# Constants on TensorE between stages, and rows scattered a step sooner, in a four-layer kernel with routed experts

## The chip, the cores and the metric

The kernel runs on one core of one Trainium2 chip. The metric is the time of one execution on the device in microseconds (us); lower is better. The engines are PE (TensorE), DVE (VectorE), ACT (ScalarE), POOL (GpSimd) and SP (SyncE, which here only issues transfers); "PEq" and "SPq" are their sequencers.

## The reference, cut to what matters

The input x is 128 sequences of 64 tokens with 128 features. Four layers follow one another. Each is a cross attention against a second input, added to x with a gate, and a feed-forward part, added with a gate:

```
x = x + tanh_gate * attention_l(layernorm(x), ctx)     # four kinds: wide heads, 16 heads of 8, masked, "stablemax"
x = x + tanh_gate * feed_forward_l(layernorm(x))
# l0: 8 experts, 128 -> 512 -> 128, one expert a token, GELU, capacity
# l1: one dense quantised network
# l2: 8 experts, two experts a token, gated SiLU, weights of the two from a softmax
# l3: 8 experts, one expert a token, ReLU, capacity, scaled by the gate's probability
```

A token's expert comes from a product of its normalised row with a small router matrix; its place ("slot") in the expert's list comes from a running count over all tokens before it.

## The kernel before, in words

The 8192 tokens are 64 tiles of 128. x stays in SBUF. There are seven long stages, one after another, each a block with a program for each engine: `attention_wide` (named l0 below), `experts` (experts0), `attention_split` three times (l1, l2, l3; l1 also carries the dense network, the `follower`), and between them `experts` again (experts2 between l2 and l3, experts3 after l3). A block ends when all engines have arrived: no engine starts the next stage before that, except for transfers of weights that were asked for early.

`attention_wide` works in 64 items of one tile, `attention_split` in 32 items of two tiles. An engine's program is a software pipeline: in step t it does part s for item t - s. In `attention_split` the parts are STAT 1, NORM 2, TURN 3, PROJ 4, SCORE 5, then PROB 6, OUT 7, STREAM 8 in l3 ("stable") and PROB 7, OUT 8, STREAM 9 in l2 ("folded") and l1. The waits between engines are on semaphores, and each engine runs its own list strictly in order.

`Router` is the tail of l0, l2 and l3. For part s of it DVE takes statistics of the finished rows (`bn_stats`, L702; `bn_aggr`, L754), POOL adds epsilon (L624) and takes the root (L629), DVE normalises (L759, written into the rows that will be sent), PE turns and scores them, and once for each batch of items DVE chooses the expert (L726 to L749), PE counts (L642 to L646), and a step later DVE turns the counts into slots (L712 to L719, the tile `put`). POOL then sends the rows to the slots in DRAM with indirect transfers (L617, one for each tile and expert of the token). A batch is 8 tiles, 4 items, in l3, and 4 tiles, 2 items, in l2. In l3 POOL's step is: eps and root for the attention's own norm (L916, L921), the same for the router (L624, L629), `combine` of the rows that came back from experts2 (L397, L401, L403), a wait for PE's output of the step (`o_filled`, L1277), then L617. In l2 L617 stands at the head of the step. In l3 DVE's step is: L1026, L674/L670, L991, L978/L982 (statistics of the item that `combine` has just finished), L1039/L1041, L966, the router's part (L702, slots, choice, L754, L759), L1061.

In l2 `Weigh` follows the last slots on DVE (L452 to L511): it turns the routing into a table of tiles and weights.

`experts` multiplies tiles of sent rows by weights: transposes (L1976), the first product (L1968; four matmuls of f32, 128 rows by 512 columns, or twice as many by 256 in experts2), the activation, and the second (L1986; matmuls of f32, 128 by 128). A matmul of f32 is two records in the trace, a transpose one.

Of the kernel before, what the change touches and what calls it, by code (L numbers as in the profile page):

```python
# [6 lines left out]
P = 128  # L7
ALU = mybir.AluOpType
# [106 lines left out]
def pipeline(eng, items, depth, emit, unroll=2):  # L115

    for t in range(items + depth - 1):
        emit(Step(eng, items, t))


def wait(eng, sem, count):
# [407 lines left out]
class Router:  # L529
# [57 lines left out]

    def depth(self):

        return 5 + self.nb  # L590

    def totals(self, nc, dve):

# [5 lines left out]
    def scatter(self, nc, pool, t, s):  # L599

        g, k = self.g, self.tiles
        out = s + 4 + self.nb
        sent_before = t.landed(out + 2, k * self.ks)

        slotted = t.batches(out - self.nb + 1 + (t.t - out) % self.nb, self.nb) if t.live(out) else None
        if t.live(out):

            if self.slots_clear and t.t == out:

                pool.wait_ge(*self.slots_clear)  # L610
            for tile in range(t.item(out) * k, t.item(out) * k + k):
                for c in range(self.ks):

                    if c == 0 and tile % k == 0:
                        wait(pool, self.put_done, slotted)
                        wait(pool, self.sent[t.par(out)], sent_before)
                    pool.indirect_dma_start(  # L617
                        self.slots, bass.IndirectOffsetOnAxis(ap=g.put[c][:, tile:tile + 1], axis=0), g.row[:, tile, self.sent_cols], None,
                        bounds_check=self.slots.shape[0] - 1, oob_is_err=False).then_inc(self.sent[t.par(out)], 16)
# [56 lines left out]
    def dve(self, nc, dve, t, s, updated, n_updated, read, n_read):  # L676
# [21 lines left out]
        if t.live(s):  # L698

            wait(dve, updated, n_updated)  # L700
            for tile in range(k):
                last = V.bn_stats(self.st[:, t.par(s), tile, :], g.x[:, bass.ds(t.item(s) * k + tile, 1), :])  # L702
            last.then_inc(self.part, 1)
        if batch4:

            link = self.chain(slotted, "slots")
            wait(dve, read, n_read)
            if self.kind == "top2":
                then(V.tensor_tensor(self.ranked[:, :, :], self.counts[:, :, :], over(self.base[:, :]), ALU.add), *link())
            for c in range(self.ks):  # L710
                src = self.ranked if self.kind == "top2" else self.counts
                then(V.tensor_tensor(self.cand[:, :, :], self.hot[c][:, :, :], src[:, :, :], ALU.mult), *link())  # L712
                then(V.tensor_reduce(self.rank[:, :], self.cand[:, :, :], AX.X, ALU.add), *link())
                if self.kind != "top2":

                    V.tensor_scalar(self.lost[:, :], self.rank[:, :], float(CAP), NOWHERE, ALU.is_gt, ALU.mult)
                    then(V.tensor_tensor(self.slot[:, :], self.rank[:, :], self.expert_base[:, :], ALU.add), *link())
                    then(V.tensor_tensor(self.rank[:, :], self.slot[:, :], self.lost[:, :], ALU.add), *link())
                last = V.tensor_copy(g.put[c][:, tiles(s + 4)], self.rank[:, :])  # L719
            last.then_inc(self.put_done, 1)  # L720
        if batch3:
# [26 lines left out]
                V.tensor_scalar(self.expert_base[:, :], self.best[:, :], -float(CAP), float(EXPERTS * CAP - 1), ALU.mult, ALU.add)  # L748
                last = V.tensor_copy(self.chosen[:, :, :], self.hot[0][:, :, :])  # L749
            last.then_inc(self.chosen_done, 1)  # L750
        if t.live(s):
            wait(dve, self.part, n0)
            for tile in range(k):
                last = V.bn_aggr(self.mv[:, t.par(s), tile, :], self.st[:, t.par(s), tile, :])  # L754
            last.then_inc(self.stats, 1)
        if t.live(s + 1):
            wait(dve, self.rstd_done, n1)
            for tile in range(k):
                last = V.tensor_scalar(  # L759
                    g.xn[:, t.item(s + 1) * k + tile, :], g.x[:, t.item(s + 1) * k + tile, :],  # L760
                    self.mv[:, t.par(s + 1), tile, 0:1], self.rstd[:, t.par(s + 1), tile:tile + 1], ALU.subtract, ALU.mult)
            last.then_inc(self.xn_done, 1)

    def chain(self, count, name):

# [13 lines left out]
def attention_split(nc, g, name, gate_col, kind, head=None, stream=None, router=None, together=None, weights=None, out=None, follow=None):  # L779
# [13 lines left out]
    with ExitStack() as ctx:  # L793
# [112 lines left out]
        @block.gpsimd  # L906
        def _(pool):
            def step(t):
                if folded:

                    wait(pool, scored, t.done(SCORE))
                    tail.scatter(nc, pool, t, T0)
                if t.live(NORM):

                    wait(pool, stats_done, t.done(NORM))
                    nc.gpsimd.tensor_tensor(var_eps[:, t.par(NORM), :], mv[:, t.par(NORM), :, 1], g.eps[:, 0:2], ALU.add).then_inc(eps_done, 1)  # L916
                if tail:
                    tail.add_eps(nc, pool, t, T0 + 1)
                if t.live(NORM):
                    wait(pool, eps_done, t.done(NORM))  # L920
                    nc.gpsimd.tensor_tensor(rstd[:, t.par(NORM), :], var_eps[:, t.par(NORM), :], g.neg_half[:, 0:2],  # L921
                                            ALU.pow).then_inc(rstd_done, 1)
                if tail:
                    tail.root(nc, pool, t, T0 + 1)
                if head and t.live(1):
                    head.combine(nc, pool, t, 1)

                if stable:

                    wait(pool, o_filled, t.done(OUT))  # L930
                    tail.scatter(nc, pool, t, T0)

            for t in range(max(ITEMS + (T0 + tail.depth() if tail else NORM + 1) - 1, FOLLOW + follower.STEPS if follower else 0)):
                if t == 10:
                    ph.clear_old()
                if follower is None or t < STEPS:
                    step(Step(pool, ITEMS, t))
                if following(t):
                    follower.gpsimd(pool, t - FOLLOW)
                    if t == FOLLOW + 16:  # L940

                        pool.wait_ge(follower.y_added, 1)
                        ph.clear_first(own)
            if tail:
                tail.finish(pool, ITEMS)

        @block.vector
        def _(dve):
# [119 lines left out]
                    tail.dve(nc, dve, t, T0, wo_drained, t.done(T0), ranks_drained, beats(t.t, T0 + 3, RANKS_BEATS))  # L1068

            for t in range(FOLLOW + follower.STEPS if follower else STEPS):  # L1070
                if t == 3:
                    prepare()
                    dve.wait_ge(ready, 1)
                if t < STEPS:
# [79 lines left out]
        def _(pe):  # L1154
# [188 lines left out]
            def handed_over(u):  # L1343
# [6 lines left out]
                if u == follower.HT_FIRST:  # L1350
                    pe.wait_ge(wo_drained, ITEMS)
                    pe.wait_ge(turned_drained, TURNED_BEATS)

            for t in range(FOLLOW + follower.STEPS if follower else STEPS):
                if t == 4:
                    pe.wait_ge(ready, 1)
                if t < STEPS:
                    step(Step(pe, ITEMS, t))
                if following(t):
                    handed_over(t - FOLLOW)  # L1360
                    follower.tensor(pe, t - FOLLOW)
            if weigh:
                weigh.tensor(nc, pe)


def attention_wide(nc, g, t_in, router, dropped, later):
# [7 lines left out]
    with ExitStack() as ctx:  # L1374
# [88 lines left out]
        def _(pool):  # L1463
            def step(t):
# [6 lines left out]
                if t.live(0):  # L1471
# [4 lines left out]
                    wait(pool, eps_done, n0)  # L1476
                    nc.gpsimd.tensor_tensor(rstd[:, t.par(0):t.par(0) + 1], var_eps[:, t.par(0):t.par(0) + 1],
                                            g.neg_half[:, 0:1], ALU.pow).then_inc(rstd_done, 1)
                tail.scatter(nc, pool, t, 8)
                tail.add_eps(nc, pool, t, 8)  # L1480
                tail.root(nc, pool, t, 8)

            ph.clear_old()
            pipeline(pool, ITEMS, 8 + tail.depth(), step, UNROLL)
# [111 lines left out]
        def _(pe):  # L1596
# [98 lines left out]
                    last.then_inc(misc_filled, 1)  # L1695

            pipeline(pe, ITEMS, DEPTH + 5, step, UNROLL)

def experts(nc, g, name, slots, rows, w1, b1, w2, b2, kind, gate_col, last=False, early=None):
# [2 lines left out]

    dynamic, gated = kind == "silu", kind == "relu"
    HALVES = 2 if dynamic else 1
    ITEMS = TOP2_TILES // 2 if dynamic else SLOT_TILES  # L1710
    WIDTH, SUBS = SLOTS // HALVES, SUB // HALVES
# [4 lines left out]
    with ExitStack() as ctx:  # L1716
# [53 lines left out]

        @block.sync
        def _(sp):
            def step(t):
                n3, n4 = t.done(3), t.done(4)

# [5 lines left out]

                if t.live(0):

                    wait(sp, xt_filled, n4)
                    wait(sp, idx_ready, n4)
                    if not dynamic:
                        wait(sp, based, n4)
                    for h in range(HALVES):
                        sp.dma_start(xs[:, t.par(0, XS), h * SUBS:h * SUBS + SUBS, :], rows_of(0, h).rearrange("(s p) d -> p s d", p=P)).then_inc(  # L1789
                            x_in[t.par(0, XS)], 16)  # L1790
                if t.live(1):

                    wait(sp, h_filled[3], t.done(1 + WS))
                    if not dynamic:
                        wait(sp, h_drained[3], n3)
                    for h in range(HALVES):
                        sp.dma_start(w1_s[:, t.par(1, WS), h, :, :], at(w1_v, expert(sp, t, 1, h))).then_inc(w1_in[t.par(1, WS)], 16)  # L1797
                    if not dynamic:
                        sp.dma_start(b1_s[:, t.par(1), :], b1[bass.ds(expert(sp, t, 1, 0), 1)].rearrange("a f c -> (a f) c")).then_inc(
                            w1_in[t.par(1, WS)], 16)  # L1800
                if t.live(2) and not dynamic:
                    load_w2(sp, t, 2)
                    sp.dma_start(b2_s[:, t.par(2), :], b2[bass.ds(expert(sp, t, 2, 0), 1)].partition_broadcast(P)).then_inc(
# [147 lines left out]
        def _(pe):  # L1951
# [38 lines left out]
            def both(t):  # L1990
                step(t)
                if early:
                    early.tensor(pe, t.t)

            pe.wait_ge(go, 1)
            pipeline(pe, ITEMS, DEPTH, both)

# [331 lines left out]
```

## Time and profile before

| | us |
|---|---|
| median of 3 runs (lowest to highest) | 2513.36 (2510.45 to 2514.68) |
| the profiled execution's own time | 2513.01 |
| its span, first to last instruction | 2511.2 |

| stage | from, us | to, us | PE busy | granted clock |
|---|---|---|---|---|
| l0 | 5.7 | 779.4 | 716.05 | 0.98 |
| experts0 | 779.4 | 919.5 | 124.56 | 0.95 |
| l1 | 919.5 | 1379.5 | 355.66 | 0.84 |
| l2 | 1379.5 | 1791.1 | 346.18 | 0.88 |
| experts2 | 1791.1 | 2020.9 | 208.76 | 0.95 |
| l3 | 2020.9 | 2366.6 | 272.94 | 0.87 |
| experts3 | 2366.6 | 2511.2 | 122.61 | 0.92 |

The granted clock is that of TensorE, as a share of 2.4 GHz; 0.50 is 1.2 GHz. The mean over the span is 0.915. A stage's time is set by whatever chain of work ends last in it, so an engine's busy share alone does not say what bounds it.

### The profile page before, as it was taken

To read this page: it belongs to the slowest core of one execution; us is meant where nothing else is said; L and a number is where in the kernel's file an instruction comes from. 1 tells how busy PE (TensorE), PEld (TensorE's weight loads), DVE (VectorE), ACT (ScalarE), POOL (GpSimd) and SP (SyncE) were. 2 spreads that over 40 slices of the span, in tenths; PEclk is the share of its full clock that TensorE was granted. 3 is DMA by queue.
4 is the path that set the end of the run, shared out by engine and by line. 5 is a ranking of instruction groups with operands and counts; after the bars stand their busy time and mean duration, and the time that the engine had idled before them with its cause. 6 is when DMAs were issued, how large, how long until landed. Compare 5 with 4: busy or idle time off the path is not lost. (4 is left out here: it accounts for less than half of the span.)

```text
span 2511.2 us, 81208 instructions
## 1 busy us (share of the span) xinstructions
PE 2146.8 (85%) x33432; PEld 1717.8 (68%) x33443; DVE 1787.9 (71%) x5105; ACT 1350.6 (54%) x2499; POOL 1157.7 (46%) x1712
## 2 busy tenths in 40 slices
PE   6999999999995969999555799998399958898597
PEld 5887878787874746777444577776399947777375
DVE  3777777777773648887896589886555559988354
ACT  3555555555551327886998455553122259979232
POOL 1333333434343541113776125555466666876444
PEclk8999999999997979998677899997699979989699
DMA  6330000000005621110000111111487622332363
GB/s 194 110 123 27 25 27 25 24 21 20 20 18 152 180 85 55 55 58 17 1 1 3 32 37 52 52 51 36 134 235 230 185 75 79 106 96 79 101 185 103
DMA packets 225233, 195.14 MB, mean 78 GB/s; under 512 B 34444, under 2 KB 197846, under 8 KB 224864
## 3 DMA queue, kind: packets, MB, share of 16 engines
q1 hardware_dynamic: 186336, 143.52, 19.6%
q0 software_dynamic: 18944, 36.98, 4.2%
q10 hardware_dynamic: 19584, 9.44, 1.3%
q8 instruction: 265, 4.34, 0.8%
q14 instruction: 104, 0.85, 0.1%
HBM read 113.53 MB, written 70.55 MB: 73 GB/s over the span
## 5 line engine op out<-in xcount | busy, mean ns | idle before, releaser
L617 POOL DMA_INDIRECT slots<-row,put x256 | 258.1, 1008 | 211.5 <-issue 131.2
L1968 PE MATMUL experts_H<-experts_xs_t,experts_w 128*128 128x256 f32 (+1 forms) x832 | 253.5, 456 | 9.9 <-DMA experts_w<-in_F_w 4.7
L1102 ACT ACTIVATE l_prob_t<-l_banks 128x512 f32<-128x512 f32 x256 | 132.2, 603 | 145.9 <-PE l_banks L1219 115.4
L1968 PEld LDWEIGHTS experts_H<-experts_xs_t,experts_w 128*128 128x128 f32 x832 | 156.7, 195 | 74.5 <-issue 54.0
L1474 POOL TENSOR_TENSOR l_var_eps<-l_mv,eps 128x1 f32<-128x1 f32 x64 | 12.1, 189 | 413.9 <-DVE l_mv L1555 413.9
L1277 PE MATMUL l_banks<-l_val,l_prob_t 128*64 128x18 f32 x5120 | 201.1, 215 | 0.0
L1277 PEld LDWEIGHTS l_banks<-l_val,l_prob_t 128*64 128x64 f32 x5120 | 190.3, 143 | 8.1 <-issue 0.7
L1510 DVE TENSOR_REDUCE l_top<-l_S 128x16 f32<-128x1024 f32 x64 | 78.3, 1224 | 161.7 <-PE l_S L1653 161.7
L1986 PE MATMUL experts_Y<-experts_w,experts_hid 128*128 128x128 f32 x1600 | 190.0, 275 | 3.5 <-DVE experts_y L1912 2.6
L1986 PEld LDWEIGHTS experts_Y<-experts_w,experts_hid 128*128 128x128 f32 x1600 | 184.3, 192 | 5.0 <-issue 4.9
L1823 POOL DMA_INDIRECT rows<-experts_y,experts_idx x144 | 139.9, 971 | 90.0 <-DVE experts_y L1908 52.9
L1012 DVE TENSOR_REDUCE l_top<-l_banks 128x32 f32<-128x2048 f32 x64 | 146.5, 2288 | 46.3 <-PE l_banks L1226 33.7
L916 POOL TENSOR_TENSOR l_var_eps<-l_mv,eps 128x2 f32<-128x2 f32 x96 | 24.3, 253 | 302.3 <-DVE l_mv L982 218.7
L1944 ACT ACTIVATE experts_hid<-experts_H,experts_b_scaled 128x512 f32<-128x512 f32 x128 | 80.0, 687 | 135.2 <-DVE experts_b_scaled L1864 115.7
L1619 PE MATMUL l_R<-l_ctx_t,l_wk 128*128 128x128 f32 x1024 | 134.2, 286 | 11.6 <-DMA l_ctx_t<-in_ctx_t 11.6
L1619 PEld LDWEIGHTS l_R<-l_ctx_t,l_wk 128*128 128x128 f32 x1024 | 122.5, 196 | 19.9 <-issue 18.3
L1469 POOL TENSOR_TENSOR l_prob<-l_prob,l_recip 128x1024 f32<-128x1024 f32 x64 | 121.3, 1895 | 24.6 <-DVE l_recip L1506 24.6
L1941 ACT ACTIVATE experts_act_gate<-experts_H 128x512 f32<-128x512 f32 x72 | 43.0, 597 | 163.3 <-PE experts_H L1968 163.3
L1567 ACT ACTIVATE l_q_t<-l_R 128x512 f32<-128x512 f32 x128 | 76.4, 597 | 96.9 <-PE l_R L1619 96.9
L1619 PE MATMUL l_R<-l_xn_t,l_wq 128*128 128x128 f32 x1024 | 126.5, 277 | 2.0 <-DVE l_xn_t L1527 2.0
L1690 PE MATMUL l_R<-l_wo,l_out_t 128*64 128x128 f32 x2048 | 126.1, 276 | 0.0
L1111 ACT ACTIVATE l_k_m<-l_banks,early_bk_masked,const_table 128x256 f32<-128x256 f32 x256 | 124.9, 595 | 0.0
(312 smaller groups left out, 5943.4 us busy)
## 6 DMA issues: line engine op xcount, KB each, us to landing
experts_w<-in_F_w SPq DMA_DIRECT2D x136, 256.0 KB
l_ctx_t<-in_ctx_t SPq DMA_DIRECT2D x96, 128.0 KB, 2.4
early_q_m<-l_q_t SPq DMA_DIRECT2D x384, 32.0 KB, 1.8
experts_xs<-slots SPq DMA_DIRECT2D x72, 132.0 KB
experts_w<-in_F_w ACTq DMA_DIRECT2D x72, 128.0 KB, 3.3
slots<-l_empty SPq DMA_DIRECT2D x16, 536.0 KB, 4.1
experts_xs<-slots SPq DMA_DIRECT2D x16, 536.0 KB
slots<-l_empty SPq DMA_DIRECT2D x16, 520.0 KB, 5.9
```

Source lines behind the costliest of these rows:

```text
L617: pool.indirect_dma_start(self.slots, bass.IndirectOffsetOnAxis(ap=g.put[c][:, tile:tile + 1], axis=0), g.row[:, tile, self.sent_cols], No ...
L1012: V.tensor_reduce(top[:, :, :].rearrange("p r a -> p (r a)"), X[:, :, :].rearrange("p r (a k) -> p (r a) k", k=64), AX.X, ALU.max).then_in ...
L1102: nc.scalar.activation(prob_t[:, t.par(PROB), r, :], Z[:, r, :], ACT.Exp).then_inc(prob_done, 1)
L1111: last = nc.scalar.activation(k_m[:, t.par(PROJ, SLOTS_QK), j, :], QK[:, 256:512], ACT.Identity, bias=bk_masked[:, j:j + 1], scale=g.const ...
L1277: last = nc.tensor.matmul(O[64 * tile:64 * tile + 64, 18 * h:18 * h + 18], term[:, t.par(OUT), h // 4, col:col + 64], val[:, t.par(OUT), t ...
L1469: nc.gpsimd.tensor_tensor(prob[:, t.par(5, 4), :, :, :], prob[:, t.par(5, 4), :, :, :], recip[:, t.par(5), :, :].unsqueeze(3).broadcast_to ...
L1619: last = nc.tensor.matmul(R[:, BANK[name], P * k:P * k + P], w[:, 4 * (c % 2) + k, :], moving, start=True, stop=True)
L1690: last = nc.tensor.matmul(MISC[64 * b:64 * b + 64, P:2 * P], out_t[:, t.par(7), k, b, :], wo_s[:, b, k, :], start=k == 0, stop=k == 7)
L1823: pool.indirect_dma_start(rows, bass.IndirectOffsetOnAxis(ap=idx[:, t.par(4, XS), k:k + 1], axis=0), y[:, t.par(4), k, :], None, bounds_ch ...
L1944: nc.scalar.activation(hid[:, t.par(2), c, :], H[:, c, :], ACT.Gelu if kind == "gelu" else ACT.Relu, bias=b1_scaled[:, t.par(2), c:c + 1], ...
L1968: last = nc.tensor.matmul(H[:, c, cols], w1_s[:, t.par(2, WS), h, c, :], xs_t[:, t.par(2), cols], start=True, stop=True)
L1986: last = nc.tensor.matmul(Y[:, P * k:P * k + P], hid[:, t.par(3), c, P * k:P * k + P], w2_s[:, t.par(3, WS), k // SUBS, c, :], start=c == ...
```

## The change

`keep_active` is a new function: a given number of matmuls of a constant by itself, into a bank that nothing reads. PE calls it before the loop of `attention_split` (16 times, in l3 40), after its steps 3 to PROB - 1 (10 each), in l2 and l3 after each of the last steps (8 each) and at the end (70 in l2, 50 in l3), at the end of l0 (34), before the first item of each `experts` stage (14), after step 1 of experts2 (12), and at the end of experts0 (45) and experts2 (55).

The router's rows are sent a step sooner: the depth is 4 + nb where it was 5 + nb (nb is the number of items in a batch), so the first item of a batch is sent in the same step in which DVE writes its slots. In l2 and l0 L617 moves to the end of POOL's step. DVE's part of the router now has L759 and L754 ahead of slots and choice. `prepare()`, DVE's clears, is called at t == 0 and not at t == 3. In experts2 SP asks for an item's first weights ahead of its rows, a step sooner.

```diff
+def keep_active(nc, g, out, count):
+    ident = g.const[:, C_IDENT:C_IDENT + P]
+    for _ in range(count):
+        nc.tensor.matmul(out, ident, ident, start=True, stop=True)
...
     def depth(self):
-        return 5 + self.nb
+        return 4 + self.nb
...
-        out = s + 4 + self.nb
+        out = s + 3 + self.nb
...
             last.then_inc(self.part, 1)
+        if t.live(s + 1):
+            wait(dve, self.rstd_done, n1)
...
+            last.then_inc(self.xn_done, 1)
+        if t.live(s):
+            wait(dve, self.part, n0)
...
+            last.then_inc(self.stats, 1)
         if batch4:
...
         if batch3:
...
-        if t.live(s):
-            wait(dve, self.part, n0)
...
-        if t.live(s + 1):
-            wait(dve, self.rstd_done, n1)
...
             def step(t):
-                if folded:
-                    wait(pool, scored, t.done(SCORE))
-                    tail.scatter(nc, pool, t, T0)
...
+                if folded:
+                    wait(pool, scored, t.done(SCORE))
                     tail.scatter(nc, pool, t, T0)
...
-                if t == 3:
+                if t == 0:
                     prepare()
...
+            IDLE = Z[:, 3, 0:P]
+            keep_active(nc, g, IDLE, 40 if head else 16)
...
+                if TURN <= t < PROB:
+                    keep_active(nc, g, IDLE, 10)
+                if t >= ITEMS + OUT - 1 and not follower:
+                    if t == ITEMS + OUT - 1:
+                        pe.wait_ge(plus_done if stable else prob_done, 4 * ITEMS)
+                    keep_active(nc, g, IDLE, 8)
...
             if weigh:
                 weigh.tensor(nc, pe)
+            if not follower:
+                keep_active(nc, g, IDLE, 70 if weigh else 50)
...
-                tail.scatter(nc, pool, t, 8)
                 tail.add_eps(nc, pool, t, 8)
                 tail.root(nc, pool, t, 8)
+                tail.scatter(nc, pool, t, 8)
...
             pipeline(pe, ITEMS, DEPTH + 5, step, UNROLL)
+            pe.wait_ge(drained["k1"], ITEMS)
+            keep_active(nc, g, R[:, 1, 0:P], 34)
...
+            def load_w1(t, s):
+                wait(sp, h_filled[3], t.done(s + WS))
+                for h in range(HALVES):
+                    sp.dma_start(w1_s[:, t.par(s, WS), h, :, :], at(w1_v, expert(sp, t, s, h))).then_inc(w1_in[t.par(s, WS)], 16)
...
                 if t.live(0):
+                    if dynamic:
+                        load_w1(t, 0)
...
+                if dynamic and t.t == 1:
+                    keep_active(nc, g, Y[:, 0:P], 12)
+            keep_active(nc, g, Y[:, 0:P], 14)
             pe.wait_ge(go, 1)
             pipeline(pe, ITEMS, DEPTH, both)
+            if not end:
+                pe.wait_ge(xt_drained, ITEMS)
+                keep_active(nc, g, X[:, 0:P], 55 if dynamic else 45)
```

## Rows read from the trace of the kernel before

**Rows 1.** Page, granted TensorE clock in 40 slices of the span, in tenths.

```profile
PEclk8999999999997979998677899997699979989699
```

**Rows 2.** Stretches, stages l2 and l3: us, busy of engines, clock, DMA share, GB/s.

```profile
1379.50:1791.10 411.60, 346.18 (x6353) 260.71 (x6353) 324.99 (x1142) 190.93 (x452) 182.50 (x256) 0.88 0.15 46
...
2020.90:2366.60 345.70, 272.94 (x4904) 224.55 (x4904) 273.58 (x809) 261.81 (x417) 237.35 (x320) 0.87 0.28 85
```

**Rows 3.** Timeline of POOL, l3, step with L719 and the next: start, us.

```profile
2158.64 0.73 POOL L403 TENSOR_TENSOR row<-row,l_term 128x256 f32<-128x256 f32 x1
...
2159.54 1.06 POOL L617 DMA_INDIRECT slots<-row,put  x1 [0.17 <-issue]
...
2163.07 0.20 POOL L624 TENSOR_TENSOR l_tail_var_eps<-l_tail_mv,eps 128x2 f32<-128x2 f32 x1 [0.96 <-DVE l_tail_mv L754]
...
2165.84 1.17 POOL L397 TENSOR_TENSOR l_term<-l_got,weight 128x256 f32<-128x256 f32 x2
...
2168.01 0.72 POOL L403 TENSOR_TENSOR row<-row,l_term 128x256 f32<-128x256 f32 x1
```

**Rows 4.** Timeline of DVE in the same stretch.

```profile
2159.40 0.49 DVE L978 BATCH_NORM_STATS2 l_st<-row 128x6 f32<-128x128 f32 x2
...
2162.67 0.17 DVE L719 CAST put<-l_rank 128x8 uint32<-128x8 f32 x1
...
2162.91 0.57 DVE L759 TENSOR_SCALAR row<-row,l_tail_mv,l_tail_rstd 128x128 f32<-128x128 f32 x2
```

**Rows 5.** Timeline, l0 to experts0.

```profile
770.12 0.19 PE L646 MATMUL l_R<-l_before,const_bf 128*128 128x32 bf16 x1
...
779.50 0.15 DVE L1838 TENSOR_SCALAR experts_gate_c<-gates 128x1 f32<-128x1 f32 x1 [7.85 <-PEq L1374]
...
785.66 5.85 PE L1968 MATMUL experts_H<-experts_xs_t,experts_w 128*128 128x512 f32 x8 [1.29 <-DMA experts_b<-in_F_b]
...
796.71 3.51 PE L1986 MATMUL experts_Y<-experts_w,experts_hid 128*128 128x128 f32 x30
```

**Rows 6.** Timeline of DVE and POOL, end of l2.

```profile
1755.89 0.60 DVE L759 TENSOR_SCALAR row<-row,l_tail_mv,l_tail_rstd 128x128 f32<-128x128 f32 x2 [1.69 <-POOL l_tail_rstd L629]
...
1770.57 0.17 DVE L719 CAST put<-l_rank 128x4 uint32<-128x4 f32 x1
...
1787.46 0.25 DVE L511 TENSOR_SCALAR weight<-l_weigh_second,gates 128x64 f32<-128x64 f32 x1
...
1788.48 0.97 POOL L617 DMA_INDIRECT slots<-row,put  x1 [0.30 <-issue]
```

**Rows 7.** Timeline, experts2's first and last matmuls.

```profile
1801.28 6.62 PE L1968 MATMUL experts_H<-experts_xs_t,experts_w 128*128 128x256 f32 x16 [4.67 <-DMA experts_w<-in_F_w]
...
1809.35 3.72 PE L1968 MATMUL experts_H<-experts_xs_t,experts_w 128*128 128x256 f32 x16 [1.01 <-DVE experts_xs_t L1878]
...
2008.83 2.02 PE L1986 MATMUL experts_Y<-experts_w,experts_hid 128*128 128x128 f32 x16 [0.88 <-DVE experts_y L1908]
```

**Rows 8.** Timeline, experts0's last matmuls; L1012 in l1.

```profile
909.73 1.50 PE L1986 MATMUL experts_Y<-experts_w,experts_hid 128*128 128x128 f32 x12
...
949.06 2.29 DVE L1012 TENSOR_REDUCE l_top<-l_banks 128x32 f32<-128x2048 f32 x1 [2.14 <-PE l_banks L1210]
...
958.12 2.29 DVE L1012 TENSOR_REDUCE l_top<-l_banks 128x32 f32<-128x2048 f32 x1 [3.15 <-PE l_banks L1210]
...
965.24 2.29 DVE L1012 TENSOR_REDUCE l_top<-l_banks 128x32 f32<-128x2048 f32 x1 [0.39 <-PE l_banks L1210]
```

**Rows 9.** Timeline of DVE, start of l2, the clears of prepare().

```profile
1382.12 0.54 DVE L953 MEMSET l_val<- 64x576 f32 x1
...
1384.04 0.49 DVE L978 BATCH_NORM_STATS2 l_st<-row 128x6 f32<-128x128 f32 x2
```

**Rows 10.** Timeline of l3: last L1277 of a step, the L617 after it.

```profile
2140.50 0.30 PE L1277 MATMUL l_banks<-l_val,l_prob_t 128*64 128x18 f32 x4
...
2141.59 1.06 POOL L617 DMA_INDIRECT slots<-row,put  x1 [0.77 <-PE l_banks L1277]
```

More of the change, by code:

```diff
@@ L703, in dve @@
             last.then_inc(self.part, 1)
+        if t.live(s + 1):
+            wait(dve, self.rstd_done, n1)
+            for tile in range(k):
+                last = V.tensor_scalar(
+                    g.xn[:, t.item(s + 1) * k + tile, :], g.x[:, t.item(s + 1) * k + tile, :],
+                    self.mv[:, t.par(s + 1), tile, 0:1], self.rstd[:, t.par(s + 1), tile:tile + 1], ALU.subtract, ALU.mult)
+            last.then_inc(self.xn_done, 1)
+        if t.live(s):
+            wait(dve, self.part, n0)
+            for tile in range(k):
+                last = V.bn_aggr(self.mv[:, t.par(s), tile, :], self.st[:, t.par(s), tile, :])
+            last.then_inc(self.stats, 1)
         if batch4:
@@ L750, in dve @@
             last.then_inc(self.chosen_done, 1)
-        if t.live(s):
-            wait(dve, self.part, n0)
-            for tile in range(k):
-                last = V.bn_aggr(self.mv[:, t.par(s), tile, :], self.st[:, t.par(s), tile, :])
-            last.then_inc(self.stats, 1)
-        if t.live(s + 1):
-            wait(dve, self.rstd_done, n1)
[L758 to L762, printed above, removed]
     def chain(self, count, name):
@@ L930, in step @@
                     wait(pool, o_filled, t.done(OUT))
+                    tail.scatter(nc, pool, t, T0)
+                if folded:
+                    wait(pool, scored, t.done(SCORE))
                     tail.scatter(nc, pool, t, T0)
@@ L1697, in _ @@
             pipeline(pe, ITEMS, DEPTH + 5, step, UNROLL)
+            pe.wait_ge(drained["k1"], ITEMS)
+            keep_active(nc, g, R[:, 1, 0:P], 34)
 def experts(nc, g, name, slots, rows, w1, b1, w2, b2, kind, gate_col, last=False, early=None):
-    dynamic, gated = kind == "silu", kind == "relu"
+    dynamic, gated, end = kind == "silu", kind == "relu", last
     HALVES = 2 if dynamic else 1
@@ L1790, in step @@
                             x_in[t.par(0, XS)], 16)
[L1791 to L1800, printed above, removed]
+                if t.live(1) and not dynamic:
+                    wait(sp, h_drained[3], n3)
+                    load_w1(t, 1)
+                    sp.dma_start(b1_s[:, t.par(1), :], b1[bass.ds(expert(sp, t, 1, 0), 1)].rearrange("a f c -> (a f) c")).then_inc(
+                        w1_in[t.par(1, WS)], 16)
                 if t.live(2) and not dynamic:
```

## The prediction

> **What bounds the kernel now.** I read the page first. Its clock line [rows 1] is at 9 tenths or full almost everywhere and falls to 6 to 8 tenths in slices near the changes of stage; the mean is 0.915, as if 427 of the 2511 us had run at half speed (0.085 / 0.5 of them). So there is something to regain, but only where TensorE at half speed is what ends last. Then I cut the span at the stages. The reader is to see in [rows 2] that PE is busy for 346 of 412 us in l2, but for only 273 of 346 in l3, where DVE (274), ACT (262) and POOL (237) are nearly as full as PE: l3 is a ring of four engines, in which none is idle long enough to swallow a late neighbour. Then I took the timeline of single engines, at one full step of l3 [rows 3, 4] and at the ends and beginnings of stages. In l3 POOL's `combine` of a step ends (L403), DVE's statistics start at once (L978), the work goes over PE and ACT and comes back to POOL as "o_filled". POOL's step is L617 twice (scatter), L916/L624/L921/L629 (eps and roots), then L397 to L403. From one L403 to the next it is 9.37 us [rows 3].
>
> The change of stage is a barrier. POOL is its last comer nearly everywhere: in l0 PE's last matmul ends at 770.31 and DVE is let go at 779.50 after 7.85 us of waiting [rows 5]; in l2 the last L617 ends at 1789.45, the last DVE instruction at 1787.71 [rows 6], and the stage ends at 1791.1 [rows 2].
>
> **The price of a constant matmul.** One is f32, 128 by 128, like those of L1986: 30 records, two for each matmul, took 3.51 us [rows 5], so 0.234 us at full clock. At half clock the double, 0.47; the same ratio shows between 6.62 and 3.72 us for the same 16 records of L1968 [rows 7].
>
> **Part 1, constants at the ends and starts of stages.** Each group has two effects: PE may reach the barrier later, and the first work of the next stage may run at full clock.
> - l0 to experts0. 34 from 770.31 would end at 778.3 if all were warm, at 786.3 if none was. They begin cold. I take 780.2 against a stage end of 779.4, +0.8 (bounds 0 and +6.9). The first L1968 took 5.85 us [rows 5] and is the same amount of columns as 3.72 [rows 7]: -2.1. Net -1.3.
> - experts0 to l1. PE's last matmul ends at 911.23 [rows 8]; 45 warm ones end at 921.8, 2.3 past the stage's end of 919.5. In l1's fill the steps of L1012 are 9.06 us and then 7.12 [rows 8]; two such steps at 1.9 less give -3.9. Net -1.6 (bounds -4 and +2.3).
> - l1 to l2. The same -3.8 at the fill. Against it stand the clears: here x is in SBUF already, so DVE's first statistics wait for the 1.92 us from 1382.12 to 1384.04 [rows 9], +1.9; and after steps 3 to 6 ten constants each, 2.3 us, which PE's waits for DVE mostly cover; I take one that is half uncovered, +1.1. Net -0.8 (bounds -4 and +3). In l1 and l3 the clears lie beside the first transfers and cost nothing; uncovered they would be another 1.9 each.
> - experts2's start. The weights are now asked for ahead of the rows. L1968 starts 4.67 us late because of experts_w [rows 7]; the weights come earlier by as much as the rows come later on the same queue, and the 12 constants stand in what is left, so I leave the start where it is, and only the clock gains: 6.62 to 3.72, -2.9 (bounds -6 and 0).
> - experts2 to l3. PE ends at 2010.85 [rows 7]; 55 constants end at 2023.7, 2.8 past 2020.9 [rows 2]. The first steps of l3 are paced by POOL's combines, so the warm clock gives back less than in l1: -2.2. Net +0.6 (bounds -3 and +3).
> - l3 to experts3: as after l0, the first L1968 at full clock, -2.1 (bounds -2.3 and 0).
>
> The rows say that after an idle stretch PE runs at 1.2 GHz and later at 2.4: the same 16 records took 6.62 and then 3.72 us [rows 7]. The Trainium skill ("TensorE: Matmul & The Clock Gate", Part 1: The HAM clock gate) says the array is throttled by default and that activity releases it; the pair agrees. It adds that the ramp penalty is under 1% of a typical span. By that last rule alone these groups could give back at most 25 us; by my rows they give back 17.
>
> **Part 2, rows sent a step sooner.** This is the part that costs. The item that is scattered is now the first of the batch whose slots DVE writes (L719) in the same step. In l3 that makes POOL, right after L403, wait for L719. Before, the scatter of that step started at 2159.54, 0.17 us after POOL's work before it [rows 3]. DVE's L978 can start only when L403 has ended (2159.40), and L719 ended at 2162.84; DVE's L759 and L754, which followed it until 2163.48 [rows 4], now stand before it, so L719 ends at 2163.48. From such a release to L617's start it is 0.79 us (2140.80 to 2141.59 [rows 10]). L617 so starts at 2164.27, 4.7 late. Behind it on POOL stand the second L617, both roots, and the combine of the next step, for which DVE waits. Given back are the 0.96 us for which L624 waited for L754 [rows 3], now done early; that leaves 3.8. The step after can save part of the 0.77 of [rows 10] (about 0.6, as 0.17 is what is left when nothing is late), and the choice step before it saves some 0.4, since the aggregate comes ahead of the choice. I take +2.8 a batch. The 32 items make eight batches, and the slots of five are written while items still come in (steps 15, 19, 23, 27 and 31): +14 (bounds: +0.8 each if the ring has slack that I don't see, +3.8 each if none; 4 and 19).
>
> In l2 POOL's sequence of instructions is the same as before, since the scatter only moves from the head of a step to the tail of the one before, and DVE waits there less than it works; nothing in the steady part. At its end, however, DVE's L759 already waits 1.69 us for POOL's root [rows 6], and POOL's root stands behind four L617. With L759 ahead of the slots, the slots are written after that wait, POOL then waits for the slots, and its next root is late: the two engines alternate instead of overlapping. Over the last three batches I estimate some 3 us for the first wait and as much again for the last batch's slots (L719 at 1770.57), from which the weighing follows (until 1787.71 [rows 6], 17.1 us of DVE). POOL's last L617 had 1.7 us more. I take +5 for the stage (bounds 0 and +9). The 70 constants behind it are 16.4 us of PE beside those 17.1 of DVE and are hidden. In l3's end the same alternation meets one batch less and a POOL that is already saturated with scatters, +2 (bounds 0 and +6); its 50 constants (11.7 us) run beside them. In l0 the batch is small and POOL is idle half the time: 0.
>
> **Sum.** -1.3 -1.6 -0.8 +5 -2.9 +0.6 +14 +2 -2.1 = +12.9. The profiled execution took 2513.0 us (its span is 2511.2), the median of the runs is 2513.4, so the two agree. 2513.0 + 12.9 = 2526.
>
> **Rivals.**
> A, faster: the new wait on L719 is hidden. The part of the ring that is ahead of POOL would need 3.8 us of slack at each batch. For it: POOL's busy share of l3 is only 237 of 346 us [rows 2]. Against it: DVE starts L978 within 0.1 us of L403's end. Then 14, 5 and 2 fall away, and the rest stays: -8.1, 2505. The deciding point is whether L617 in those steps can start within 1 us of L403. The Trainium skill (same page, HAM oscillation) speaks for this side: each idle stretch between bursts of matmuls throttles the array and the ramp is paid again, so filling them should pay; the trace agrees with the throttling and no row here prices it beyond the terms above.
> B, no change: the waits cost half of what I take (about 1.4 a batch and +2 at l2's end): +12.9 -7 -3 = +2.9, 2516. For it: the step ahead of each such step is the one in which DVE also makes the choice, and a late POOL may be caught up there.
> C, slower still: the constants don't hold the clock up. The 34 of l0 then cost the whole +6.9 (6.1 more), and if only a third of the 17.1 us of clock gains is lost, that is 6 more: 2538. The point from which it decides is the duration of the first L1968 after a group, 5.85 or 3.7. Against it: nothing is denser than matmuls back to back, and 1809.35 ran at 3.72 after 8 us of looser work [rows 7].
>
> **Chances and range.** The forecast (waits cost 8 us or more) 0.50, A 0.25, B 0.15, C 0.10. A measurement here tells 0.2%, 5 us, from no change: faster 0.25, same 0.15, slower 0.60. The range reaches from a little under A to C, 2502 to 2538; the forecast's own is 2519 to 2534.
>
> **What would show it.** Right: in l3, at each L719, L617 idle for about 4 us and released by DVE's put, and the next L978 waiting some 3 us longer for L403; L759 ahead of L719; l2 about 5 us longer from its last L1277 to the weighing's end; first L1968 near 3.7 in all three expert stages. Wrong: l3 no longer than 346 us, or a half-clock stretch still over the expert stages' starts, or PE's sequencer named as the last comer at barriers with more than 3 us.

## The result, and the profile after

| | before | changed |
|---|---|---|
| median, us | 2511.9 (2508.7 to 2514.7, 4 runs) | 2545.4 (2540.4 to 2555.4, 4 runs) |
| ratio | | 1.015, 95% interval 1.0124 to 1.0175 |
| profiled execution: span, granted clock | 2511.2, 0.915 | 2546.3, 0.942 |

The change makes the kernel about 33 us slower. The direction was forecast; the size (+13) was not, and 2545 lies outside the range of 2502 to 2538. TensorE's mean clock rose all the same. The stages of the two profiled executions, cut at the first instruction after each barrier:

| stage | before, us | changed, us | difference | sum of my terms |
|---|---|---|---|---|
| l0 | 779.5 | 779.6 | +0.1 | +0.8 |
| experts0 | 140.2 | 140.1 | -0.1 | +0.2 |
| l1 | 459.9 | 454.9 | -5.0 | -3.9 |
| l2 | 411.7 | 423.6 | +11.9 | +4.2 |
| experts2 | 229.6 | 231.1 | +1.5 | -0.1 |
| l3 | 345.8 | 372.9 | +27.1 | +13.8 |
| experts3 | 144.5 | 144.0 | -0.5 | -2.1 |

The stretches of the two stages that grew most answer to [rows 2] (us; busy of PE, PEld, DVE, ACT and POOL; clock, DMA share, GB/s):

```profile
1374.62:1798.25 423.63, 388.80 (x6717) 307.26 (x6718) 324.56 (x1142) 191.29 (x452) 181.95 (x256) 0.92 0.15 45
...
2029.40:2402.27 372.87, 321.63 (x5257) 273.22 (x5257) 264.85 (x810) 262.30 (x417) 225.47 (x320) 0.89 0.26 79
```

PE's busy time grew by 49 us in l3. The constants are 33 of them (no_constants, below, has 288.25); DVE's, ACT's and POOL's busy time fell or stayed. So the 27 us are not more work on those three. The timeline of POOL in the changed kernel at the step that answers to [rows 3] (new line numbers: L624 is the scatter that was L617, L410 is the combine's L403):

```profile
2169.68 0.73 POOL L410 TENSOR_TENSOR row<-row,l_term 128x256 f32<-128x256 f32 x1
2176.58 1.23 POOL L624 DMA_INDIRECT slots<-row,put  x1 [6.17 <-issue]
...
2182.81 0.72 POOL L410 TENSOR_TENSOR row<-row,l_term 128x256 f32<-128x256 f32 x1
```

And DVE's there (L985 was L978, L738 was L719), which answers to [rows 4]:

```profile
2171.36 0.47 DVE L985 BATCH_NORM_STATS2 l_st<-row 128x6 f32<-128x128 f32 x2
...
2175.57 0.17 DVE L738 CAST put<-l_rank 128x8 uint32<-128x8 f32 x1
...
2183.57 0.49 DVE L985 BATCH_NORM_STATS2 l_st<-row 128x6 f32<-128x128 f32 x2 [2.80 <-POOL row L410]
```

POOL idles 6.17 us for the slots, which are written at 2175.74; the scatter starts 0.84 later. From one L410 to the next it is 13.13 us where it was 9.37 [rows 3]. The wait has "issue" as its releaser: what ends it is a semaphore wait of the queue that the profile doesn't resolve, and only DVE's timeline shows which. The wait is longer than forecast (4.7 late, so 4.9 of idle) for a reason that the same rows show. The forecast let DVE's statistics start at once after the combine; here L410 ends at 2170.41 and L985 starts 0.95 later, because DVE is still at earlier parts of its own list. From L985's start to the slots it is then 4.38, where the forecast had 4.08.

Two steps later PE itself is late: POOL's scatter in that step waits for it. That row, then the stretch's clock:

```profile
2198.31 1.06 POOL L624 DMA_INDIRECT slots<-row,put  x1 [6.42 <-PE l_banks L1284]
```

```profile
2184.13:2201.19 17.06, 16.01 (x187) 12.91 (x187) 10.36 (x33) 8.80 (x15) 9.45 (x13) 0.50 0.23 71
```

The granted clock falls to 0.50, 1.2 GHz, 7.6 us after the late scatter began, and stays there for 17 us, of which PE is busy for 16.0. Before the fall PE had been busy for 10.9 of the 13.1 us of the stalled step, and in the whole of the next step it is for 6.0 of 8.3. The step after that took 14.26 us where it was 8.60. The kernel before has such a stretch too, without any wait for slots, around a step of 13.32 us:

```profile
2233.90:2250.90 17.00, 16.24 (x187) 12.90 (x187) 11.88 (x37) 8.89 (x16) 9.72 (x14) 0.50 0.33 100
```

At l3's end, timelines of DVE, POOL and PE in the changed kernel (L714 was L759, L668 scores the router's rows, L125 is the constant):

```profile
2378.76 0.60 DVE L714 TENSOR_SCALAR row<-row,l_tail_mv,l_tail_rstd 128x128 f32<-128x128 f32 x2 [4.14 <-POOL l_tail_rstd L636]
```

```profile
2375.39 1.04 POOL L624 DMA_INDIRECT slots<-row,put  x1 [5.89 <-issue]
...
2389.32 0.97 POOL L624 DMA_INDIRECT slots<-row,put  x1 [2.89 <-issue]
```

```profile
2379.97 3.62 PE L125 MATMUL l_banks<-const_table 128*128 128x128 f32 x16
2383.38 0.86 PE L668 MATMUL l_banks<-l_router_w,l_tail_xn_t 128*128 128x8 f32 x4
...
2386.87 14.98 PE L125 MATMUL l_banks<-const_table 128*128 128x128 f32 x132
2402.27 3.36 PE L125 MATMUL experts_Y<-const_table 128*128 128x128 f32 x28 [0.41 <-PEq L800]
```

POOL waits for slots (5.89), DVE for POOL's root (4.14), eight constants at half clock (3.62) stand ahead of the scores that DVE needs for the next choice, and POOL waits again (2.89). Then 66 constants in a row end 0.4 us before everybody is let go: PE is the last comer at this barrier, POOL's last scatter having ended 3.0 before it (1.8 was usual).

Two of three starts became warm. The first products of experts0 and experts2 are to be set beside [rows 5] (5.85) and [rows 7] (6.62); that of experts3, the last row, took 5.76 before and is still mostly at half clock:

```profile
785.74 3.67 PE L1990 MATMUL experts_H<-experts_xs_t,experts_w 128*128 128x512 f32 x8 [1.85 <-DMA experts_b<-in_F_b]
...
1810.18 3.62 PE L1990 MATMUL experts_H<-experts_xs_t,experts_w 128*128 128x256 f32 x16
...
2408.44 5.37 PE L1990 MATMUL experts_H<-experts_xs_t,experts_w 128*128 128x512 f32 x8 [1.80 <-DMA experts_b<-in_F_b]
```

### The profile page after: what moved, and what is told of

It reads as the page before. It is cut to its first block and busy times, and to the rows that moved or that the text cites. A ratio compares the mean times of both kernels' runs of the same rounds, so it can differ in the third digit from the quotient of the medians.

```text
span 2546.3 us, 83624 instructions
## 1 busy us (share of the span) xinstructions
PE 2279.6 (90%) x34647; PEld 1859.2 (73%) x34647; DVE 1777.0 (70%) x5105; ACT 1351.6 (53%) x2499; POOL 1146.7 (45%) x1712
## 5 line engine op out<-in xcount | busy, mean ns | idle before, releaser
L624 POOL DMA_INDIRECT slots<-row,put x256 | 259.1, 1012 | 272.1 <-issue 210.2
L1990 PE MATMUL experts_H<-experts_xs_t,experts_w 128*128 128x256 f32 (+1 forms) x832 | 247.9, 448 | 6.4 <-DMA experts_b<-in_F_b 3.7
L1845 POOL DMA_INDIRECT rows<-experts_y,experts_idx x144 | 140.2, 973 | 90.2 <-DVE experts_y L1930 53.5
L1636 PE MATMUL l_R<-l_ctx_t,l_wk 128*128 128x128 f32 x1024 | 134.1, 285 | 10.4 <-DMA l_ctx_t<-in_ctx_t 10.4
L1636 PEld LDWEIGHTS l_R<-l_ctx_t,l_wk 128*128 128x128 f32 x1024 | 122.5, 196 | 18.7 <-issue 17.1
```

The costliest lines, as they stand in the source:

```text
L624: pool.indirect_dma_start(self.slots, bass.IndirectOffsetOnAxis(ap=g.put[c][:, tile:tile + 1], axis=0), g.row[:, tile, self.sent_cols], No ...
L1636: last = nc.tensor.matmul(R[:, BANK[name], P * k:P * k + P], w[:, 4 * (c % 2) + k, :], moving, start=True, stop=True)
L1845: pool.indirect_dma_start(rows, bass.IndirectOffsetOnAxis(ap=idx[:, t.par(4, XS), k:k + 1], axis=0), y[:, t.par(4), k, :], None, bounds_ch ...
L1990: last = nc.tensor.matmul(H[:, c, cols], w1_s[:, t.par(2, WS), h, c, :], xs_t[:, t.par(2), cols], start=True, stop=True)
```

## The experiments

Eleven kernels were run. Ratios are to the kernel before on the same chip. The stages come from each kernel's one profiled execution, cut like the table above. "Last combine" is the start of the last L410 (L403) after the start of l3; "rest" is what follows until the stage's end; all columns from l2 on are in us. A profiled execution can lie up to 11 us from its kernel's median: those of late_scatter and best took 2499.3 and 2487.0, 10 and 9 below it, that of late_no_eights 2519.0, 11 above. So stages of single profiles are compared with that in mind, and the ratios decide.

| kernel | median, us | ratio (95%) | l2 | experts2 | l3 | last combine | rest | half clock in l3 |
|---|---|---|---|---|---|---|---|---|
| before | 2511.9 | | 411.7 | 229.6 | 345.8 | 262.1 | 83.7 | 93 |
| changed | 2545.4 | 1.015 (1.0124-1.0175) | 423.6 | 231.1 | 372.9 | 276.2 | 96.7 | 85 |
| no_constants | 2539.7 | 1.0115 (1.0067-1.0163) | 419.9 | 228.5 | 369.8 | 276.2 | 93.6 | 134 |
| only_constants | 2522.1 | 1.0028 (1.0006-1.005) | 415.8 | 229.3 | 352.7 | 262.4 | 90.3 | 65 |
| late_scatter | 2509.1 | 0.9998 (0.9969-1.0026) | 419.8 | 231.4 | 330.7 | 246.9 | 83.8 | 14 |
| old_order | 2550.7 | 1.0157 (1.0109-1.0205) | 415.2 | 229.6 | 380.8 | 286.7 | 94.1 | 113 |
| order_only | 2506.4 | 0.9983 (0.9969-0.9998) | 413.7 | 228.4 | 332.7 | 247.9 | 84.8 | 73 |
| late_no_constants | 2506.2 | 0.9973 (0.9956-0.999) | 419.9 | 228.3 | 333.8 | 248.9 | 84.9 | 78 |
| late_no_eights | 2508.1 | 0.9992 (0.9975-1.001) | 419.3 | 231.2 | 343.6 | 252.7 | 90.9 | 62 |
| late_starts | 2499.4 | 0.9952 (0.9938-0.9967) | 420.0 | 228.8 | 333.8 | 247.1 | 86.7 | 54 |
| l3_late | 2511.1 | 1.0002 (0.9984-1.0019) | 415.4 | 232.0 | 341.1 | 251.5 | 89.6 | 44 |
| late_starts_clears3 | 2502.5 | 0.9972 (0.9956-0.9988) | 419.5 | 229.1 | 333.1 | 249.8 | 83.3 | 53 |
| best | 2496.4 | 0.9951 (0.9936-0.9966) | 407.7 | 227.1 | 334.8 | 250.6 | 84.2 | 58 |

The expectations below give l2 for some kernels 2.1 us shorter (417.7, 417.8, 421): they count it from DVE's first statistics, which with the clears at t == 0 come 2.1 us after the barrier. The table counts from the barrier for all.

**no_constants.** The changed kernel; `keep_active` issues nothing.

```diff
-    for _ in range(count):
+    for _ in range(0):
         nc.tensor.matmul(out, ident, ident, start=True, stop=True)
```

> The changed kernel without a single constant matmul (the waits around them stay). Theory 1 (POOL waits for the slots of the same step, in l3's steps and at the ends of l2 and l3) expects the loss to stay: l3 still near 365 us or more, L978's put steps still near 12.5 us instead of 9.4, total 2535 to 2545 against about 2512 before. Theory 2 (the constants stand in PE's queue ahead of the router's small matmuls and pull the clock about) expects nearly all of it gone: l3 near 348, total about 2515.

l3 is 369.8 and the ratio 1.0115: theory 1 holds, theory 2 falls. The last combine is at 276.2 with constants and without them, and the steps with slots took 12.3 to 13.1 us.

**only_constants.** The kernel before, with all calls of `keep_active`.

> The kernel before with all the constant matmuls and nothing else. Theory 1 expects 2508 to 2518, that is no more than 5 us either way: the fills of l1 and l2 and the first products gain 1 to 2 us each, the eight after each last step and the groups before the barriers cost 3 to 6 in all. Theory 2 expects 2530 or more, with l3 at 360 or more.

1.0028: a small loss. The median, 2522.1, is 4 above the range of theory 1 and 9 above that of the kernel before, and far from theory 2. The last combine does not move (262.4 against 262.1); what grew are l2, by 4.1, and l3's rest, by 6.6.

**late_scatter.** The changed kernel, scatter a step later; in l2 and l0 its call goes back to its old place in POOL's step, too (not shown).

```diff
-        return 4 + self.nb
+        return 5 + self.nb
...
-        out = s + 3 + self.nb
+        out = s + 4 + self.nb
```

> The changed kernel with the rows scattered a step later again (depth 5 + nb, and L617's call back at the head of the step in l2 and l0); DVE keeps the new order, constants, clears and weights stay. Theory 1 expects l3's put steps back at 9.4 us and l3 at 345 to 352; at l2's end DVE's normalised rows still stand ahead of the slots, but POOL does not wait for them in the same step, so l2 near 414; total 2510 to 2520. Theory 2 expects no change from the changed kernel, about 2540.

The total is as theory 1 has it, but l3 is 330.7, not 345 to 352, and l2 419.8, not 414. In these profiled executions something in the change saves 15 us in l3, and the sooner scatter costs not 27 but 42 there; the medians of the two kernels are 36 us apart. The stretch of l3:

```profile
2024.60:2355.30 330.70, 293.28 (x5257) 252.84 (x5257) 264.80 (x809) 262.19 (x417) 229.85 (x320) 0.98 0.29 89
```

POOL in the step of the choice and after it:

```profile
2150.44 0.73 POOL L410 TENSOR_TENSOR row<-row,l_term 128x256 f32<-128x256 f32 x1
...
2154.43 0.20 POOL L631 TENSOR_TENSOR l_tail_var_eps<-l_tail_mv,eps 128x2 f32<-128x2 f32 x1
...
2159.01 0.73 POOL L410 TENSOR_TENSOR row<-row,l_term 128x256 f32<-128x256 f32 x1
...
2167.97 0.72 POOL L410 TENSOR_TENSOR row<-row,l_term 128x256 f32<-128x256 f32 x1
...
2169.25 1.06 POOL L624 DMA_INDIRECT slots<-row,put  x1 [0.56 <-issue]
...
2176.42 0.73 POOL L410 TENSOR_TENSOR row<-row,l_term 128x256 f32<-128x256 f32 x1
```

POOL's epsilon no longer waits for the aggregate in the step of the choice; in the kernel before that row is

```profile
2153.82 0.21 POOL L624 TENSOR_TENSOR l_tail_var_eps<-l_tail_mv,eps 128x2 f32<-128x2 f32 x1 [1.23 <-DVE l_tail_mv L754]
```

The step is 8.57 us (2150.44 to 2159.01), where it was 9.90, and the step of the slots 8.96, where it was 9.37.

**old_order.** The changed kernel, DVE's slots and choice ahead of aggregate and normalised rows again.

> The changed kernel with DVE's old order (slots and choice ahead of aggregate and normalised rows), scatter a step sooner, all else as changed. Theory 1 splits here: if waiting for the slots in l3 is the large term, l3 stays within 5 us of the changed kernel's 373 (slots 0.6 us earlier in five steps, but the 1.4 us given back in the choice steps are lost too), and l2 gets shorter by 4 to 8, since the last slots no longer stand behind POOL's root; total 2532 to 2545. If the order on DVE was the large term, the total falls to 2520 or less.

1.0157, the median 6 above the range that I gave, and l3 at 380.8, 8 longer than in the changed kernel; l2 8 shorter, which is no more than one program's l2 differs from itself (l3_late). Waiting for the slots is the large term. I had expected 5 us at most in l3; the new order is worth more than that there.

**order_only.** The kernel before, with these two blocks moved:

```diff
+        if t.live(s + 1):
+            wait(dve, self.rstd_done, n1)
...
+        if t.live(s):
+            wait(dve, self.part, n0)
...
         if batch4:
...
         if batch3:
```

> The kernel before with DVE's new order alone (normalised rows, then aggregate, ahead of slots and choice), no other part of the change. The stretch of l3 in the late-scatter run was 331 us against 346 before, with the constants in. If the order is what gives that back, l3 here is 325 to 332 and the total 2495 to 2502, since l2's end costs 2 to 4. The rival (the gain needs the clock that the constants hold up, or the clears) expects l3 at 343 or more and a total within 5 us of before.

l3 is 332.7, so the order alone gives 13 us in the profiled execution, with 73 us of it at half clock: neither constants nor clears are needed. The total missed: 2506.4 against 2495 to 2502. The medians differ by 5.5 us, and the ratio's interval (0.9969 to 0.9998) is the number to keep; it only just excludes no change.

**late_no_constants.** Order, clears at t == 0 and weights first; late scatter, no constants.

> DVE's new order, the clears at the first step and experts2's weights ahead of its rows, without constants and without the sooner scatter. If clears and weights cost nothing, the total is that of the order alone within 3 us, with l2 and experts2 as before (412 to 415, 229). The rival: asking for the weights first makes experts2 start later, experts2 at 231 or more as in the changed kernel, and the clears make l2's fill 1 to 2 us longer.

0.9973 beside 0.9983: clears and weights cost nothing that shows. experts2 is 228.3, so the 231 of the changed kernel is not the order of its transfers. l2 is 419.9, longer than expected.

**late_no_eights.** late_scatter without the eight constants after each of the last steps.

```diff
-                    keep_active(nc, g, IDLE, 8)
+                    keep_active(nc, g, IDLE, 0)
```

> The late-scatter kernel without the eight constants after each of the last steps of l2 and l3; all other constants stay. If they stand in the way of the router's small matmuls there (3.6 us at half clock in front of L668 in the changed kernel's trace), l2 gets shorter by 2 to 4 and l3 by 2 to 5 against 417.7 and 330.7. If they only fill gaps, both stay within 1 us.

Inconclusive: 0.9992 against 0.9998, intervals that overlap; l2 hardly moved, and l3's rest is longer, not shorter.

**late_starts.** Without the groups that end a stage, too (70, 50, 34, 55, 45).

> As the kernel without the eights, and also without the groups that end l0, experts0, l2, experts2 and l3 (34, 45, 70, 55, 50), so constants only at starts and in the fills. PE was the last comer at the barriers with those groups (0.1 to 0.4 us before each, POOL 0.6 to 2.6 us earlier than usual), so taking them out should bring each barrier 0.6 to 2.5 us forward, 7 us in all; against that the next stage starts at half speed again, 2 us each in four places. I expect the total within 4 us of the kernel without the eights. The rival (the warm start is worth more than the barrier) expects it 5 us or more slower.

0.9952, 8.7 us below late_no_eights in the median: more than I expected. The ending groups cost. experts2 is back at 228.8, so its 231 was the 55 constants ahead of the barrier, in which PE was the last comer. And no start went cold: the first products of the three expert stages took 3.70, 3.62 and 3.70 us with the 14 constants behind the barrier alone (likewise in the last two kernels below), where the changed kernel, with both groups, has 5.37 in experts3. They began 0.7, 2.1 and 0.6 us later after the barrier than in the kernel before. That of experts0:

```profile
784.88 3.70 PE L1990 MATMUL experts_H<-experts_xs_t,experts_w 128*128 128x512 f32 x8 [0.86 <-DVE experts_xs_t L1900]
```

**l3_late.** The changed kernel, scatter late in l3 alone.

```diff
-        return 4 + self.nb
+        return (5 if self.together == 8 else 4) + self.nb
...
-        out = s + 3 + self.nb
+        out = s + (4 if self.together == 8 else 3) + self.nb
```

> The changed kernel with the scatter a step later again in l3 alone; in l2 and l0 it stays a step sooner. If the loss lies in l3's wait for the slots, l3 is 331 to 335 and the total 2498 to 2508; l2 stays at 421, because there the order of DVE and the sooner scatter are both still in. If the sooner scatter in l2 and l0 were a large part, the total would stay above 2515.

The total is that of late_scatter within the intervals (1.0002, 0.9998). So the whole cost of the sooner scatter that a median can show lies in l3. The total of 2498 to 2508 was missed by 3. l3 itself is 341 and not 331 to 335: with the instructions of late_scatter's l3 it lost 4 us in its first twelve steps and 6 in the rest. l2 is 415.4, with the very instructions that took 423.6 in the changed kernel: l2's length in one execution is uncertain by 8 us, l3's by 10.

**late_starts_clears3** and **best.** The first puts the clears back to t == 3, the second in addition keeps the old order on DVE in l2.

```diff
+        if self.kind != "top2":
+            self.normalise(nc, dve, t, s)
         if batch4:
...
             last.then_inc(self.chosen_done, 1)
+        if self.kind == "top2":
+            self.normalise(nc, dve, t, s)
```

> The kernel with constants at the starts alone and the late scatter, and with the clears back at t == 3. Both runs with the clears at the first step and the late scatter show l2 at 417.8, that with the order alone 413.7. If the clears are the difference, l2 is 412 to 414 here and the total 2492 to 2498; if not, l2 stays at 418 and the total at 2499.

> As the run before, and DVE's new order only in l0 and l3; in l2 slots and choice come first, as before. At l2's end the slots then no longer stand behind POOL's root: l2 1 to 2 us shorter than in the run before (411 to 413), total 2490 to 2497. The rival (the end of l2 was only the clears') expects no difference between the two.

The clears were not the cause (419.5 against 420.0, ratio 0.9972, no better than with early clears). The last kernel is at 0.9951, 12 us faster than before, its l2 at 407.7. From late_starts (0.9952) it can't be told by the ratio. Its lower l2 shows nothing for the old order either: from the last item's finished row to the end of l2 it is 40.9 against 41.5 us in the run before, where 1 to 2 were expected, and the other 11 lie among the 32 items, where one program differed from itself by 8.

## Why the prediction was wrong

The sum was +12.9 and the profiled executions differ by 35.0. The two terms that failed most are in l3 (+13.8 forecast, +27.1 measured) and in l2 (+4.2 and +11.9).

1. **The mechanism of part 2 was right, its size in l3 was wrong, and that the last combine came out at +14 is luck.** It moved from 262.1 to 276.2, +14.1, against +14 forecast. But the forecast was 2.8 for each of five batches. Against late_scatter, which differs in the scatter alone, it is 29.3; a gain of 15.2 that I had not forecast (point 3) hides the rest. The five steps with slots took 12.98, 13.13, 12.25, 12.26 and 13.08 us, there 8.81 to 8.97: 19.1 in all, so 3.8 a batch, the upper bound that I had given and not taken. Two things made it so: DVE's statistics did not start at once after the combine (0.95 later), and of the "0.6" that the next step should give back 0.1 came (0.4 once).
2. **Not in the forecast at all: what the stall does to PE's clock.** Four steps, each the second behind a stall, took 10.5, 14.3, 9.6 and 10.6 us against 8.5 to 8.6: 10.8 us, the rest of the 29.3. In the 14.3 one TensorE is at 0.50 for 10.0 us; the other three run at full clock, each behind a step in which the clock stood at 0.50, and PE is busy for 10.3, 8.8 and 10.4 us of them, where it is for 7.6 to 8.0 in late_scatter: it catches up. The longer the stretch at 0.50, the longer the step: 3.4 us of it cost 1.1, 6.8 and 6.9 cost 2.0 each, 17.1 cost 5.7. Two more stretches of 3.4 fall just ahead of steps in which POOL waits for slots anyway. With the same constants and the scatter late, none of these stretches is there; without constants and the scatter soon, they are there with the same lengths and the same four steps (10.3, 14.3, 9.6, 10.5). So they come with the stall, and the constants do not touch them: none is issued in those steps. I had treated clock and waits as separate terms. That the sizes are the clock's is read from the traces; no kernel held the clock up in those steps.
3. **Not in the forecast either: the new order on DVE is a gain of its own.** I had given it 0.4 a batch, for the aggregate in the step of the choice. The five choice steps were 1.3 to 1.5 shorter (6.9 us in the changed kernel, 6.8 in order_only). In order_only the steps of the slots give 2.0 more, and 4.9 is one step of 13.3 us in the kernel before, the one with 17 us at half clock around it, which other executions need not have. Together the order alone brings the last combine from 262.1 to 247.9 in these two profiles, and the median down by 5.5.
4. **The end of l3, +2, was mis-sized.** The rest went from 83.7 to 96.7. All three kernels with the sooner scatter in l3 have 93.6 to 96.7, the others 83.3 to 90.9; without constants it is 93.6 with the scatter soon and 84.9 with it late, so about 9 belongs to the scatter. What the constants do there is not settled: they add 3.1 here, 6.6 to the kernel before and -1.1 with the scatter late, while the same l3 program took 83.8 once and 89.6 once. I had called the 50 hidden and given the eights no term. POOL "already saturated with scatters" was the wrong reason: its waits of 5.89 and 2.89 stand ahead of the last 16 scatters.
5. **The end of l2, +5, was right in sign, its reason was half right, and the larger part of l2's growth was not at its end.** From the last item's finished row (L966) to the stage's end it was 39.5 us before and is 42.8 in the changed kernel and 42.9 in l3_late. With the scatter late it is 43.3, and without constants 41.5 (soon) and 41.6 (late): so the sooner scatter costs nothing there, the new order about 2 (41.4 in order_only, 39.9 in old_order), and the constants that I had called hidden about 1.5. The other 8.6 of l2's 11.9 came among its 32 items, where I had forecast -0.8 in all; 2.1 are the clears, 1.9 forecast. The same program took 8.3 less in those items in l3_late, so the rest may be the difference between two executions; its cause stays open.
6. **Clears and weights ahead of rows:** small, as forecast (0.9973 against 0.9983 with the order alone).
7. **The starts became warm in two of three places, and it was worth less than I said.** The first products took 3.67 and 3.62, as forecast, but 5.37 in experts3, which gained 0.5 and not 2.1. experts0 did not get shorter, because the 45 constants at its end hold the barrier for 2.0 us, the forecast's 2.3. In experts2 the first product began 11.9 us after the barrier and not 10.0, behind the 12 constants, and POOL's last transfer ended 4.1 ahead of the next barrier and not 1.6, so the stage lost 1.5. In l3 the -2.2 did not come: the fourteenth combine starts 91.6 us after the stage's start, 91.2 before. l1 gained 5.0 against 3.9. All constants together cost 0.28% on the kernel before; those at the starts alone did no harm (0.9952 against 0.9973 without any, intervals that overlap).

So the clauses "+2.8 a batch" and "+2 at l3's end" failed, with the 0.4 for the order, the items of l2, and the hidden constants. One reading was loose: 6.62 to 3.72 is a ratio of 1.78 and not of two. The prices themselves held: eight constants took 3.62 us at half clock, 0.45 each, and 66 took 14.98 at full clock, 0.23 each. Rivals A and B fell: the wait was not hidden or halved. C fell at its deciding point in two of three places, and in l1 and l2 the constants did take half-clock time away (150 to 102 us and 97 to 65); in experts3 and in l3's steps they did not.

## What to carry to other kernels

Where several engines form a ring, give a stall its full size unless a row shows the slack that takes it, and add what PE's clock does in the steps after it. An engine's work that nobody waits for in this step (slots and choice) belongs behind the work that somebody waits for (aggregate and normalised rows); in l3 that gained, at the end of l2 it cost 2 us. Sending early is worth nothing if the sender is in the ring and the receiver is a stage away. Constants that keep TensorE warm belong behind the barrier, where it waits for data, and not ahead of it, where it can become the last comer: the 14 behind the barrier were enough for warm first products, and the groups ahead of it cost 8.7 us in the median.

## What the runs showed of the hardware

- A higher mean clock can go with a longer time: 0.942 at 2546 us against 0.915 at 2511.
- With the same constants the clock in l3 follows the waits: 14 us at half clock with the late scatter, 85 with the sooner one. The Trainium skill ("TensorE: Matmul & The Clock Gate", HAM oscillation) describes this as idle stretches that throttle the array again and again; the runs agree that the clock falls again and again, and here it did so in the step after POOL's waits for slots. The kernel before shows that such a wait is not needed for it: 17.0 us at 0.50 from 2233.9 on.
- Half clock cost time only in some places. order_only spends 73 us of l3 at 0.50, late_scatter 14. Of the 73, 24 are the first of the stage and 42 lie in the rest after the last combine, which is 1.0 us longer; one stretch of 3.4 lies in the steps with a full ring, and the step behind it took 9.51 us and not 8.56, which is the 1 us by which the last combine is later.
